# Time mixing: six element-wise passes per chunk moved from VectorE to GpSimd, and the second norm's passes reordered

## The chip, the cores and the metric

The kernel runs on 1 core of a Trainium2 chip. The metric is the device time of one execution in microseconds (us): median of several runs. Engines in the rows: PE is TensorE (matmul), DVE is VectorE, ACT is ScalarE, POOL is GpSimd, SP is SyncE.

## The reference, cut to what matters

The program is a chain of twelve sublayers over an activation of 32 batches, 64 tokens and 256 channels. The change is in the eighth, time mixing (an RWKV attention). It starts with a plain layer norm of the running activation `x`, whose output is `h` in the kernel and `hidden_state` in this cut of the reference:

```python
def _reference_tuple_inner(hidden_state, ln_w, ln_b, Wk, Wv, Wr, Wo, mix_k, mix_v, mix_r, time_decay, current_token_weight):
    residual = hidden_state
    x = _layer_norm(hidden_state, ln_w, ln_b)
    sx = concatenate([zeros, x[:, :-1, :]], axis=1)
    xk, xv, xr = (sx + mix * (x - sx) for mix in (mix_k, mix_v, mix_r))
    r = sigmoid(xr @ Wr.T); k = xk @ Wk.T; v = xv @ Wv.T
    wkv = _wkv(k, v, time_decay, current_token_weight)
    return residual + (r * wkv) @ Wo.T

def step(carry, kv):            # one token of _wkv
    num, den, norm = carry
    kt, vt = kv
    ct = curr_w + kt
    cn = maximum(ct, norm)
    e_prev, e_cur = exp(norm - cn), exp(ct - cn)
    out = (e_prev * num + e_cur * vt) / (e_prev * den + e_cur)
    dpn = decay + norm          # decay = -exp(time_decay)
    new_norm = maximum(dpn, kt)
    e_d, e_k = exp(dpn - new_norm), exp(kt - new_norm)
    return ((e_d * num + e_k * vt, e_d * den + e_k, new_norm), out)
```

The result is added to the running activation `x`, together with `h`.

## The kernel before, in words

Channels lie on the 128 partitions in H2 = 2 halves, the 32 x 64 tokens on the free axis. `time_mixing` (line 1962) works in NCH = 4 chunks of CH = 512 tokens, so that one element-wise pass over a chunk is 128 x 1024. All tensors are f32.

For each chunk c the work is:

- First norm (`ln1`, class `Norm`, line 152), from `k.x` to `k.h`: mean by a matmul (line 171), `centre` on VectorE (line 184, reads PSUM), `squares` on ScalarE (line 197), variance by a matmul (line 179), `inverse` on ScalarE (lines 203 and 205), `scale` on VectorE (line 190). Second norm (`ln2`), the same from `k.h` to `y0`; `affine` on ScalarE (line 2073) writes `yp`.
- `mix` on VectorE: the difference of neighbouring tokens (line 2158, tm_diff), then six instructions (line 2165) that give three mixed inputs, two per projection.
- `project` on TensorE (line 2023): keys, values and gate, each in two halves through one PSUM tile `p_p`; each half waits until ScalarE has copied the same half of the projection before (`keep`, lines 2081, 2085, 2087). The sigmoid of the gate needs two table loads around it (lines 2091 and 2093).
- On VectorE a scan of the maxima (line 2196), four shifts (lines 2201, 2202, 2208, 2209) and the joined maximum (line 2204); on ScalarE an exponential of each shift (lines 2099, 2101). The shifts share one semaphore, which counts four per chunk.
- On VectorE: product 0 of exps and values (line 2214), the scan of the denominator (line 2215), the first norm's scale, the scan of the numerator (line 2220), product 1 (line 2222), two value passes (lines 2225, 2226), `ln_in` (line 2228) and the last sum (line 2230).
- ScalarE takes the logarithm of `ln_in` and its inverse (lines 2138, 2140). VectorE multiplies by the gate (line 2238) and by the inverse into tm_weighted (line 2243).
- `project_out` on TensorE: four records (two matmuls) of the identity by `h` (line 2034), which add the residual, then eight with the output weights (line 2038). VectorE adds the result to `k.x` (line 2171) one chunk later.

A matmul of f32 with 512 columns shows as two records here, so a projection of a chunk (three inputs) is 24 records.

The order of each engine's work is written out by hand in the four blocks of `time_mixing`; instructions of one engine run in that order, and a wait holds back all that stands behind it. Work runs ahead: in the body of chunk c, VectorE mixes chunk c + 1 and runs both norms of chunk c + 2, and TensorE projects chunk c + 1. GpSimd has only three small memsets at the start (lines 2148 to 2150). SyncE loads the weights once. Stage state (tiles `diff`, `yp`, `kp`, `vv`, `rr`, `fo`) has two buffers each.

Of the kernel before, what the change touches and what calls it, by code (L numbers as in the profile page):

```python
# [13 lines left out]
ALU = mybir.AluOpType  # L14
# [6 lines left out]
ts = bass.ts  # L21
# [1940 lines left out]
def time_mixing(k):  # L1962
# [4 lines left out]
    with ExitStack() as ctx:  # L1967
        k.stage += 1
        k.prefix = "tm_"
        sem = semaphores(nc, ctx, k.prefix, "pad affine diff mixed proj kept decay constant joined shifts exps scanned den num "  # L1970
                                            "values weighed ln_in logged inverse fused out added" + Norm.SEMS + Norm.SEMS2)
# [43 lines left out]
        @block.tensor  # L2015
        def _(pe):
            def project(c, n):
                pe.wait_ge(sem["mixed"], 3 * c + n + 1)
                for o in range(H2):
                    if 3 * c + n >= 1:  # L2020
                        pe.wait_ge(sem["kept"], H2 * (3 * c + n - 1) + o + 1)
                    for a in range(H2):
                        mm = pe.matmul(p_p[:, o, :], w[:, n, a, ts(o, P)], mx[:, n, a, :], start=a == 0, stop=a == H2 - 1)
                    mm.then_inc(sem["proj"], 1)

            def mean2(c):
# [24 lines left out]
            for n in range(3):  # L2051
                project(0, n)
            for c in range(NCH):
                if c + 2 < NCH:
                    ln1.var(pe, c + 2)
                if c + 1 < NCH:
                    for n in range(3):
                        project(c + 1, n)
                if c + 3 < NCH:
                    ln1.mean(pe, c + 3)  # L2060
                if c + 2 < NCH:
                    mean2(c + 2)
                    ln2.var(pe, c + 2)
                project_out(c)

        @block.scalar
        def _(act):
# [27 lines left out]
            def exponential(c, n):  # L2095
                act.wait_ge(sem["shifts"], 4 * c + n + 1)
# [22 lines left out]
            for c in range(NCH):  # L2119
                if c + 2 < NCH:  # L2120
                    ln1.squares(act, c + 2)
                if c == 0:
                    act.wait_ge(sem["constant"], 1)
                elif c + 1 < NCH:
                    ln2.inverse(act, c + 1)
                exponential(c, 0)
                if 1 <= c < NCH - 1:
                    affine(c + 1)
# [12 lines left out]
                if c + 2 < NCH:  # L2141
                    ln2.squares(act, c + 2)
# [3 lines left out]
        @block.gpsimd  # L2146
        def _(g):
            g.memset(yp[:, :, :, :, 0:1], 0.0).then_inc(sem["pad"], 1)
            g.memset(kp[:, :, :, :, 0:1], NEG).then_inc(sem["pad"], 1)
            g.memset(run[:, :, 0:1], 0.0).then_inc(sem["pad"], 1)  # L2150

        @block.vector
        def _(v):
            def mix(c):
                v.wait_ge(sem["affine"], c + 1)
                if c >= 2:
                    v.wait_ge(sem["mixed"], 3 * (c - 1))
                v.tensor_tensor(tok(flat(diff[:, c % 2, :, :])), yp[:, c % 2, :, :, 1:S1].rearrange("p o b t -> p (o b) t"),
                                yp[:, c % 2, :, :, 0:S].rearrange("p o b t -> p (o b) t"), ALU.subtract).then_inc(sem["diff"], 1)
# [30 lines left out]
            for c in range(NCH):  # L2190
# [7 lines left out]
                if 1 <= c < NCH - 1:  # L2198
                    ln2.scale(v, c + 1)
# [9 lines left out]
                v.tensor_tensor(tok(expo[3]), keys(c), tok(latest), ALU.subtract).then_inc(sem["shifts"], 1)  # L2209
# [3 lines left out]
                v.wait_ge(sem["kept"], H2 * (3 * c + 2))  # L2213
                v.tensor_tensor(prod[:, 0, :], expo[1], flat(vv[:, c % 2, :, :]), ALU.mult).then_inc(sem["weighed"], 1)
# [12 lines left out]
                v.wait_ge(sem["values"], 4 * c + 2)  # L2227
# [3 lines left out]
                if c + 2 < NCH:  # L2231
                    v.wait_ge(sem["affine"], c + 1)
# [729 lines left out]
```

## Time and profile before

| what | us |
|---|---|
| median of 3 runs | 3419.49 (3416.7 to 3420.05) |
| the profiled execution | 3442.91 |
| its span | 3441.1 |
| PE busy in the span | 2825.3 (82%) |
| DVE busy | 1875.5 (55%) |
| ACT busy | 1394.7 (41%) |
| POOL busy | 921.0 (27%) |

Time mixing takes about 1952 to 2116 us of the span. The shares are means over twelve stages with different limits, so what bounds this one must be read from its own stretch. The chain of work that ended last, as the profile prints it, covers other stages only. The granted clock (PEclk) is TensorE's, as a share of 2.4 GHz.

### The profile page before, as it was taken

The numbers are of one execution on the slowest core, as the hardware profiler recorded it, in microseconds if no ns is written. First come the engines' busy times: TensorE is split into PE (matmuls) and PEld (weight loads), VectorE is DVE, ScalarE is ACT, GpSimd is POOL, SyncE is SP. The second block draws the span as 40 slices with busy tenths as digits, with TensorE's granted clock in tenths as the row PEclk, the third lists the DMA queues.
The fourth block names the chain that finished last, engine by engine and source line by source line (L and its number), as shares of the span: only waits on it lengthen the run. The fifth ranks groups of instructions, "written<-read, shape, count | busy, mean of one in ns | idle before, by whom it ended". The sixth has DMA issues, their size and how long they took to land. (4 is left out here: it accounts for less than half of the span.)

```text
span 3441.1 us, 45938 instructions
## 1 busy us (share of the span) xinstructions
PE 2825.3 (82%) x16624; PEld 1693.8 (49%) x16624; DVE 1875.5 (55%) x2398; ACT 1394.7 (41%) x2464; POOL 921.0 (27%) x733
## 2 busy tenths in 40 slices
PE   7999986899987988789979875587896777785894
PEld 5888864356554647433336432244532333342784
DVE  2333334222258827334479697868755999962341
ACT  3333335121255526222265453465565555530222
POOL 0111100300214512000005300004503999945005
PEclk9999997999998989899989997788998899887997
DMA  6000002311110000200000000000001221222223
GB/s 220 0 0 0 0 7 104 119 43 45 52 40 1 2 20 2 79 1 0 18 1 2 14 0 0 1 19 2 2 25 64 86 85 73 86 74 72 79 83 104
DMA packets 88659, 139.96 MB, mean 41 GB/s; under 512 B 12081, under 2 KB 70449, under 8 KB 83890
## 3 DMA queue, kind: packets, MB, share of 16 engines
q1 hardware_dynamic: 80818, 116.73, 10.0%
q0 software_dynamic: 7680, 20.98, 2.0%
q8 instruction: 114, 1.87, 0.2%
q14 instruction: 47, 0.39, 0.0%
HBM read 105.57 MB, written 32.11 MB: 40 GB/s over the span
## 5 line engine op out<-in xcount | busy, mean ns | idle before, releaser
L2673 PE MATMUL ssm_p_y<-ctxT,ident 128*128 128x512 f32 x512 | 271.3, 685 | 90.0 <-POOL ctxT L2710 82.9
L2719 POOL TENSOR_TENSOR h<-ssm_u,ssp_bc 128x1024 f32<-128x1024 f32 x128 | 297.9, 2361 | 0.0
L2695 ACT ACTIVATE ssm_p_h<-ssp_delta,ss_decay 128x256 f32<-128x256 f32 x512 | 213.7, 463 | 193.7 <-DVE ctxT L2753 165.0
L2673 PEld LDWEIGHTS ssm_p_y<-ctxT,ident 128*128 128x128 f32 x512 | 108.5, 219 | 244.2 <-issue 116.3
L2750 DVE TENSOR_TENSOR_SCAN ssm_p_h<-ssm_p_h,h 128x1024 f32<-128x1024 f32 x88 | 201.2, 2286 | 6.7 <-POOL h L2719 6.4
L559 DVE TENSOR_REDUCE xw_nmax<-xw_p_s 128x8 f32<-128x1024 f32 x32 | 39.2, 1225 | 237.1 <-PE xw_p_s L490 237.1
L580 POOL TENSOR_TENSOR xw_prob<-xw_prob,xw_rsum 128x1024 f32<-128x1024 f32 x32 | 60.7, 1896 | 370.7 <-DVE xw_rsum L566 370.7
L1329 POOL MEMSET ctxT<- 128x512 f32 x3 | 1.6, 526 | 567.2 <-POOLq L61 567.2
L467 PE MATMUL xw_p_q<-h,xw_m_h 128*128 (+1 forms) x1024 | 117.0, 275 | 1.3 <-PEq L61 1.3
L475 PE MATMUL xw_p_q<-xw_u,xw_vo_h 128*128 128x128 f32 x1024 | 117.1, 275 | 0.7 <-ACT xw_u L540 0.7
L475 PEld LDWEIGHTS xw_p_q<-xw_u,xw_vo_h 128*128 128x128 f32 x1024 | 115.6, 192 | 2.2 <-ACT xw_u L540 2.2
L467 PEld LDWEIGHTS xw_p_q<-h,xw_m_h 128*128 128x128 f32 x1024 | 115.6, 192 | 1.7 <-issue 1.7
L2753 DVE TENSOR_TENSOR ctxT<-ssm_p_h,ssp_bc 128x1024 f32<-128x1024 f32 x88 | 107.7, 1224 | 3.0
L1920 ACT ACTIVATE lmm_hidden<-lmm_p_h,vecs 128x512 f32<-128x512 f32 x64 | 43.5, 687 | 153.6 <-PE lmm_p_h L1880 108.1
L1086 POOL DMA_INDIRECT L0f_rows<-L0f_rows_out,L0f_slots x32 | 30.3, 947 | 264.4 <-DMA L0f_rows_out<-L0b_y 250.1
L1086 POOL DMA_INDIRECT L3f_rows<-L3f_rows_out,L3f_slots x48 | 45.4, 947 | 203.2 <-DMA L3f_rows_out<-L3b_y 182.4
L1048 DVE TENSOR_TENSOR L0f_hidden<-L0f_silu,L0b_p_u 128x512 f32<-128x512 f32 x39 | 26.8, 688 | 124.1 <-PE L0b_p_u L992 124.1
L2710 POOL TENSOR_TENSOR ctxT<-ctxT,ssp_bc 128x1024 f32<-128x1024 f32 x40 | 94.1, 2353 | 0.5 <-DVE ctxT L2746 0.4
L2746 DVE TENSOR_TENSOR_SCAN ctxT<-ssm_p_h,h 128x1024 f32<-128x1024 f32 x40 | 91.2, 2281 | 1.4 <-POOL h L2719 1.0
L1949 DVE TENSOR_TENSOR lmm_hidden<-lmm_hidden,lm_weights 128x512 f32<-128x512 f32 x64 | 44.1, 689 | 87.6 <-ACT lmm_hidden L1920 87.6
L1508 POOL TENSOR_TENSOR L1xb_prob<-L1xb_prob,L1xb_rsum 128x896 f32<-128x896 f32 x64 | 65.4, 1042 | 65.5 <-DVE L1xb_rsum L1487 65.5
L1508 POOL TENSOR_TENSOR L3xb_prob<-L3xb_prob,L3xb_rsum 128x896 f32<-128x896 f32 x64 | 65.4, 1042 | 65.2 <-DVE L3xb_rsum L1487 65.2
(650 smaller groups left out, 6771.0 us busy)
## 6 DMA issues: line engine op xcount, KB each, us to landing
ssp_bc<-ss_bc_rows SPq DMA_DIRECT2D x32, 1024.0 KB, 4.7
expert_rows_in<-xw_blank SPq DMA_DIRECT2D x1, 6912.0 KB, 22.0
L3b_x<-expert_rows_in SPq DMA_DIRECT2D x54, 128.0 KB, 2.0
L3f_rows_out<-L3b_y SPq DMA_DIRECT2D x54, 128.0 KB, 1.7
L0b_x<-expert_rows_in SPq DMA_DIRECT2D x39, 128.0 KB, 2.0
L0f_rows_out<-L0b_y SPq DMA_DIRECT2D x39, 128.0 KB, 1.7
L0f_wg<-in_L_ffn_gate SPq DMA_DIRECT2D x9, 512.0 KB, 10.1
L0f_wu<-in_L_ffn_up SPq DMA_DIRECT2D x9, 512.0 KB, 10.0
```

The lines of the kernel that those rows point to most:

```text
L467: mm = pe.matmul(p_q5[:, q % 2, h % 4 // 2, :, h % 2, :], m_h[:, h, a, :], k.h[:, a, ts(i, P)], start=h % 4 == 0 and a == 0, stop=a == H2 ...
L475: mm = pe.matmul(p_q[:, 0, ts(o, P)], vo_h[:, h, ts(o, P)], us[:, h, :], start=h == 0 and o == 0, stop=h == NH - 1, skip_group_check=True)
L580: g.tensor_tensor(prob[:, :, :], prob[:, :, :], bcast(rsum[:, 1, :], 2, S2), ALU.mult).then_inc(sem["normed"], 1)
L1086: g.indirect_dma_start(out=back[:, t % RG, j, :], out_offset=None, in_=rows_out[:, :], in_offset=bass.IndirectOffsetOnAxis(ap=slots[:, j, ...
L1508: scaled = g.tensor_tensor(prob[:, w, :, :, s0:s1], prob[:, w, :, :, s0:s1], bcast(rsum[:, 1, w, m, :, :], 3, s1 - s0), ALU.mult)
L2673: mm = pe.matmul(p_y[:, 2 * half:2 * half + 2, :].rearrange("p e t -> p (e t)"), k.ident[:, :], weighed[s % RING][:, ts(half, CH)], start= ...
L2695: i = act.activation(p_h[:, s % 2, ts(e, CT)], delta[:, e, ts(c, CT)], ACT.Exp, scale=decay[:, 1, E4 * s + e:E4 * s + e + 1])
L2710: g.tensor_tensor(tiles(weighed[s % RING]), tiles(weighed[s % RING]), bcast(bcs[:, s // QUARTER, 1, s % QUARTER, :], 1, E4), ALU.mult).the ...
L2719: g.tensor_tensor(tiles(drive[s % RING]), u[:, c % 2, :, :], bcast(bcs[:, s // QUARTER, 0, s % QUARTER, :], 1, E4), ALU.mult).then_inc(sem ...
L2746: v.tensor_tensor_scan(weighed[s % RING], p_h[:, s % 2, :], drive[s % RING], 0.0, ALU.mult, ALU.add).then_inc(sem["scanned"], 1)
L2750: v.tensor_tensor_scan(p_h[:, s % 2, :], p_h[:, s % 2, :], drive[s % RING], 0.0, ALU.mult, ALU.add).then_inc(sem["scanned"], 1)
L2753: v.tensor_tensor(tiles(weighed[s % RING]), tiles(p_h[:, s % 2, :]), bcast(bcs[:, s // QUARTER, 1, s % QUARTER, :], 1, E4), ALU.mult).then ...
```

## The change: what it does

Six passes run on GpSimd: the difference, the fourth shift (with a semaphore of its own, shift3; the other three keep `shifts`, which now counts three per chunk), both products, a new pass `residual` that adds `h` to `k.x`, and a new pass `gated` that multiplies the gate by the inverse, in place, so that VectorE has one pass (tm_weighted) for the two before. The identity matmuls are gone. The second norm's `centre` moves ahead of the value passes, its `scale` from the next chunk's body to just before tm_weighted; ScalarE's `squares`, `inverse` and `affine` of that norm move around the logarithm and ahead of the gate; TensorE computes the second norm's mean and variance ahead of the first norm's next mean.

```diff
@@ tensor @@
             def project_out(c):
+                pe.wait_ge(sem["fused"], c + 1)
                 if c >= 1:
                     pe.wait_ge(sem["added"], c)
                 for o in range(H2):
-                    pe.matmul(p_y[:, o, :], k.ident[:, :], k.h[:, o, ts(c, CH)], start=True, stop=False, skip_group_check=True)
-                pe.wait_ge(sem["fused"], c + 1)
-                for o in range(H2):
                     for a in range(H2):
...
-                if c + 3 < NCH:
-                    ln1.mean(pe, c + 3)
                 if c + 2 < NCH:
                     mean2(c + 2)
                     ln2.var(pe, c + 2)
+                if c + 3 < NCH:
+                    ln1.mean(pe, c + 3)
                 project_out(c)
@@ scalar @@
                 if c == 0:
                     act.wait_ge(sem["constant"], 1)
-                elif c + 1 < NCH:
-                    ln2.inverse(act, c + 1)
                 exponential(c, 0)
-                if 1 <= c < NCH - 1:
-                    affine(c + 1)
                 exponential(c, 1)
...
                     keep(c + 1, 1)
+                if c + 2 < NCH:
+                    ln2.squares(act, c + 2)
                 act.wait_ge(sem["ln_in"], c + 1)
                 act.activation(expo[2], expo[2], ACT.Ln).then_inc(sem["logged"], 1)
                 act.wait_ge(sem["logged"], c + 1)
                 act.activation(expo[2], expo[2], ACT.Exp, scale=-1.0).then_inc(sem["inverse"], 1)
                 if c + 2 < NCH:
-                    ln2.squares(act, c + 2)
+                    ln2.inverse(act, c + 2)
+                    affine(c + 2)
                 if c + 1 < NCH:
                     gate(c + 1)
@@ gpsimd @@
+            def difference(c):
+                g.wait_ge(sem["affine"], c + 1)
+                if c >= 2:
+                    g.wait_ge(sem["mixed"], 3 * (c - 1))
+                g.tensor_tensor(tok(flat(diff[:, c % 2, :, :])), yp[:, c % 2, :, :, 1:S1].rearrange("p o b t -> p (o b) t"),
+                                yp[:, c % 2, :, :, 0:S].rearrange("p o b t -> p (o b) t"), ALU.subtract).then_inc(sem["diff"], 1)
+
+            def residual(c):
+                g.wait_ge(sem["ln_normed"], c + 1)
+                g.tensor_tensor(k.x[:, :, ts(c, CH)], k.x[:, :, ts(c, CH)], k.h[:, :, ts(c, CH)], ALU.add).then_inc(sem["residual"], 1)
...
+            difference(0)
+            residual(0)
+            residual(1)
+            for c in range(NCH):
+                if c + 1 < NCH:
+                    difference(c + 1)
+                g.wait_ge(sem["joined"], c + 1)
+                g.tensor_tensor(tok(expo[3]), keys(c), tok(latest), ALU.subtract).then_inc(sem["shift3"], 1)
+                g.wait_ge(sem["exps"], 4 * c + 2)
+                g.wait_ge(sem["kept"], H2 * (3 * c + 2))
+                g.tensor_tensor(prod[:, 0, :], expo[1], flat(vv[:, c % 2, :, :]), ALU.mult).then_inc(sem["weighed"], 1)
+                g.wait_ge(sem["exps"], 4 * c + 4)
+                g.tensor_tensor(prod[:, 1, :], expo[3], flat(vv[:, c % 2, :, :]), ALU.mult).then_inc(sem["weighed"], 1)
+                if c + 2 < NCH:
+                    residual(c + 2)
+                g.wait_ge(sem["inverse"], c + 1)
+                g.wait_ge(sem["kept"], H2 * (3 * c + 3))
+                g.tensor_tensor(flat(rr[:, c % 2, :, :]), flat(rr[:, c % 2, :, :]), expo[2], ALU.mult).then_inc(sem["gated"], 1)
@@ vector @@
             def add(c):
                 v.wait_ge(sem["out"], c + 1)
+                v.wait_ge(sem["residual"], c + 1)
...
-                if 1 <= c < NCH - 1:
-                    ln2.scale(v, c + 1)
...
-                v.tensor_tensor(tok(expo[3]), keys(c), tok(latest), ALU.subtract).then_inc(sem["shifts"], 1)
...
-                v.tensor_tensor(prod[:, 0, :], expo[1], flat(vv[:, c % 2, :, :]), ALU.mult).then_inc(sem["weighed"], 1)
...
                 v.tensor_tensor_scan(latest, expo[0], prod[:, 0, :], 0.0, ALU.mult, ALU.add).then_inc(sem["num"], 1)
+                if c + 2 < NCH:
+                    v.wait_ge(sem["affine"], c + 1)
+                    ln2.centre(v, c + 2)
                 v.wait_ge(sem["exps"], 4 * c + 4)
-                v.tensor_tensor(prod[:, 1, :], expo[3], flat(vv[:, c % 2, :, :]), ALU.mult).then_inc(sem["weighed"], 1)
...
-                if c + 2 < NCH:
-                    v.wait_ge(sem["affine"], c + 1)
-                    ln2.centre(v, c + 2)
                 if c >= 1:
                     add(c - 1)
-                v.wait_ge(sem["kept"], H2 * (3 * c + 3))
-                v.wait_ge(sem["values"], 4 * c + 3)
-                v.tensor_tensor(expo[0], expo[0], flat(rr[:, c % 2, :, :]), ALU.mult).then_inc(sem["values"], 1)
-                v.wait_ge(sem["inverse"], c + 1)
-                v.wait_ge(sem["values"], 4 * c + 4)
+                if c + 2 < NCH:
+                    ln2.scale(v, c + 2)
+                v.wait_ge(sem["gated"], c + 1)
+                v.wait_ge(sem["values"], 3 * c + 3)
                 if c >= 2:
                     v.wait_ge(sem["out"], c - 1)
-                v.tensor_tensor(flat(fo[:, c % 2, :, :]), expo[0], expo[2], ALU.mult).then_inc(sem["fused"], 1)
+                v.tensor_tensor(flat(fo[:, c % 2, :, :]), expo[0], flat(rr[:, c % 2, :, :]), ALU.mult).then_inc(sem["fused"], 1)
```

## Rows read from the trace of the kernel before

**Rows 1.** Busy time by stretch: one window per chunk, by the end of its last pass.
```profile
1982.40:2022.20 39.80, 30.28 (x64) 12.85 (x64) 37.16 (x36) 22.14 (x30) 0.00 (x0) 0.91 0.00 0
2022.20:2056.80 34.60, 26.83 (x52) 11.18 (x51) 32.78 (x30) 19.64 (x27) 0.00 (x0) 0.85 0.00 0
2056.80:2086.80 30.00, 19.28 (x39) 7.67 (x38) 29.45 (x28) 15.62 (x21) 0.00 (x0) 0.89 0.00 0
2086.80:2110.00 23.20, 6.09 (x11) 2.61 (x12) 23.01 (x18) 7.91 (x9) 0.00 (x0) 0.65 0.00 0
```

**Rows 2.** Timeline of VectorE: start us, duration us, line, operation, idle before and releaser.
```profile
2000.54 4.07 DVE L2165 SCALAR_TENSOR_TENSOR tm_mixed<-tm_diff,vecs,tm_y 128x512 f32<-128x512 f32 x6
...
2020.93 1.23 DVE L2243 TENSOR_TENSOR tm_weighted<-tm_exps 128x1024 f32<-128x1024 f32 x1
...
2035.20 4.06 DVE L2165 SCALAR_TENSOR_TENSOR tm_mixed<-tm_diff,vecs,tm_y 128x512 f32<-128x512 f32 x6
...
2055.61 1.23 DVE L2243 TENSOR_TENSOR tm_weighted<-tm_exps 128x1024 f32<-128x1024 f32 x1
...
2085.54 1.23 DVE L2243 TENSOR_TENSOR tm_weighted<-tm_exps 128x1024 f32<-128x1024 f32 x1
...
2104.06 1.23 DVE L2228 TENSOR_TENSOR tm_exps<-tm_exps 128x1024 f32<-128x1024 f32 x1
2105.21 1.22 DVE L2230 TENSOR_TENSOR tm_exps<-tm_exps,tm_products 128x1024 f32<-128x1024 f32 x1
...
2108.78 1.23 DVE L2243 TENSOR_TENSOR tm_weighted<-tm_exps 128x1024 f32<-128x1024 f32 x1
```

**Rows 3.** Timeline of TensorE, merged records, same columns as rows 2.
```profile
1985.24 10.54 PE L2023 MATMUL tm_p_p<-tm_mixed,tm_w 128*128 128x512 f32 x24 [2.58 <-DVE tm_mixed L2165]
2000.24 3.78 PE L179 MATMUL tm_ln_p_var<-tm_ln_square,mean_ones 128*128 128x512 f32 x4 [4.46 <-ACT tm_ln_square L197]
2003.82 11.11 PE L2023 MATMUL tm_p_p<-tm_mixed,tm_w 128*128 128x512 f32 x24
...
2036.67 8.80 PE L2023 MATMUL tm_p_p<-tm_mixed,tm_w 128*128 128x512 f32 x13 [5.29 <-DVE tm_mixed L2165]
...
2050.03 1.88 PE L171 MATMUL tm_lm_p_mean<-h,mean_ones 128*128 128x512 f32 x4
...
2107.61 3.62 PE L2034 MATMUL tm_p_y<-h,ident 128*128 128x512 f32 x4 [17.08 <-DVE x L2171]
2111.06 3.60 PE L2038 MATMUL tm_p_y<-tm_weighted,tm_w 128*128 128x512 f32 x8
```

**Rows 4.** Groups of GpSimd by line and shape, whole program.
```profile
L2719 POOL TENSOR_TENSOR h<-ssm_u,ssp_bc 128x1024 f32<-128x1024 f32 x128 | 297.9, 2361 | 0.0
...
L580 POOL TENSOR_TENSOR xw_prob<-xw_prob,xw_rsum 128x1024 f32<-128x1024 f32 x32 | 60.7, 1896 | 370.7 <-DVE xw_rsum L566 370.7
L1508 POOL TENSOR_TENSOR L1xb_prob<-L1xb_prob,L1xb_rsum 128x896 f32<-128x896 f32 x32 | 53.8, 1683 | 65.5 <-DVE L1xb_rsum L1487 65.5
...
L1508 POOL TENSOR_TENSOR L1xb_prob<-L1xb_prob,L1xb_rsum 128x128 f32<-128x128 f32 x32 | 12.9, 402 | 0.0
...
L1493 POOL MEMSET L1xb_vx<- 128x1024 f32 x1 | 1.0, 951 | 65.9 <-POOLq L61 65.9
```

**Rows 5.** State-space stage, timeline of GpSimd, then of VectorE.
```profile
2636.66 2.35 POOL L2701 TENSOR_TENSOR ssm_u<-ssp_delta,ss_xc 128x1024 f32<-128x1024 f32 x1 [61.32 <-POOLq L61]
...
2639.28 9.26 POOL L2719 TENSOR_TENSOR h<-ssm_u,ssp_bc 128x1024 f32<-128x1024 f32 x4
...
2641.73 2.30 DVE L2750 TENSOR_TENSOR_SCAN ssm_p_h<-ssm_p_h,h 128x1024 f32<-128x1024 f32 x1 [5.83 <-POOL h L2719]
...
2645.20 2.28 DVE L2746 TENSOR_TENSOR_SCAN ctxT<-ssm_p_h,h 128x1024 f32<-128x1024 f32 x1
```

**Rows 6.** Timeline of ScalarE: affine of chunk 1, logarithm of chunk 0.
```profile
1997.72 1.52 ACT L2073 ACTIVATE tm_y<-tm_y,vecs 128x512 f32<-128x512 f32 x2
...
2015.94 1.06 ACT L2138 ACTIVATE tm_exps<-tm_exps 128x1024 f32<-128x1024 f32 x1 [3.82 <-DVE tm_exps L2228]
```

More of the change, by code:

```diff
@@ L1969, in time_mixing @@
         k.prefix = "tm_"
-        sem = semaphores(nc, ctx, k.prefix, "pad affine diff mixed proj kept decay constant joined shifts exps scanned den num "
-                                            "values weighed ln_in logged inverse fused out added" + Norm.SEMS + Norm.SEMS2)
+        sem = semaphores(nc, ctx, k.prefix, "pad affine diff mixed proj kept residual decay constant joined shifts shift3 exps scanned den num "
+                                            "values weighed ln_in logged inverse gated fused out added" + Norm.SEMS + Norm.SEMS2)
         s_w = nc.alloc_semaphore("tm_weights_loaded")
@@ L2033, in project_out @@
                 for o in range(H2):
-                    pe.matmul(p_y[:, o, :], k.ident[:, :], k.h[:, o, ts(c, CH)], start=True, stop=False, skip_group_check=True)
-                pe.wait_ge(sem["fused"], c + 1)
-                for o in range(H2):
                     for a in range(H2):
-                        mm = pe.matmul(p_y[:, o, :], w[:, 3, a, ts(o, P)], fo[:, c % 2, a, :], start=False, stop=a == H2 - 1, skip_group_check=True)
+                        mm = pe.matmul(p_y[:, o, :], w[:, 3, a, ts(o, P)], fo[:, c % 2, a, :], start=a == 0, stop=a == H2 - 1)
                 mm.then_inc(sem["out"], 1)
@@ L2095, in exponential @@
             def exponential(c, n):
-                act.wait_ge(sem["shifts"], 4 * c + n + 1)
+                if n < 3:
+                    act.wait_ge(sem["shifts"], 3 * c + n + 1)
+                else:
+                    act.wait_ge(sem["shift3"], c + 1)
                 if n in (0, 3):
@@ L2150, in _ @@
             g.memset(run[:, :, 0:1], 0.0).then_inc(sem["pad"], 1)
+            g.wait_ge(sem["pad"], 1)
+            difference(0)
[16 more added lines that the diff above has]
+                g.tensor_tensor(flat(rr[:, c % 2, :, :]), flat(rr[:, c % 2, :, :]), expo[2], ALU.mult).then_inc(sem["gated"], 1)
         @block.vector
@@ L2154, in mix @@
             def mix(c):
-                v.wait_ge(sem["affine"], c + 1)
[L2156 to L2159, printed above, removed]
                 v.wait_ge(sem["diff"], c + 1)
@@ L2212, in _ @@
                 v.wait_ge(sem["exps"], 4 * c + 2)
-                v.wait_ge(sem["kept"], H2 * (3 * c + 2))
-                v.tensor_tensor(prod[:, 0, :], expo[1], flat(vv[:, c % 2, :, :]), ALU.mult).then_inc(sem["weighed"], 1)
                 v.tensor_tensor_scan(run[:, 1, 1:N + 1], expo[0], expo[1], 0.0, ALU.mult, ALU.add).then_inc(sem["den"], 1)
@@ L2218, in _ @@
                 v.wait_ge(sem["weighed"], 2 * c + 1)
-                v.wait_ge(sem["shifts"], 4 * c + 4)
+                v.wait_ge(sem["shifts"], 3 * c + 3)
                 v.tensor_tensor_scan(latest, expo[0], prod[:, 0, :], 0.0, ALU.mult, ALU.add).then_inc(sem["num"], 1)
+                if c + 2 < NCH:
+                    v.wait_ge(sem["affine"], c + 1)
+                    ln2.centre(v, c + 2)
                 v.wait_ge(sem["exps"], 4 * c + 4)
-                v.tensor_tensor(prod[:, 1, :], expo[3], flat(vv[:, c % 2, :, :]), ALU.mult).then_inc(sem["weighed"], 1)
                 v.wait_ge(sem["den"], c + 1)
@@ L2226, in _ @@
                 v.tensor_tensor(expo[2], expo[2], run[:, 1, 0:N], ALU.mult).then_inc(sem["values"], 1)
-                v.wait_ge(sem["values"], 4 * c + 2)
+                v.wait_ge(sem["values"], 3 * c + 2)
                 v.tensor_tensor(expo[2], expo[2], expo[3], ALU.add).then_inc(sem["ln_in"], 1)
@@ L2230, in _ @@
                 v.tensor_tensor(expo[0], expo[0], prod[:, 1, :], ALU.add).then_inc(sem["values"], 1)
-                if c + 2 < NCH:
-                    v.wait_ge(sem["affine"], c + 1)
-                    ln2.centre(v, c + 2)
                 if c >= 1:
                     add(c - 1)
-                v.wait_ge(sem["kept"], H2 * (3 * c + 3))
-                v.wait_ge(sem["values"], 4 * c + 3)
-                v.tensor_tensor(expo[0], expo[0], flat(rr[:, c % 2, :, :]), ALU.mult).then_inc(sem["values"], 1)
-                v.wait_ge(sem["inverse"], c + 1)
-                v.wait_ge(sem["values"], 4 * c + 4)
+                if c + 2 < NCH:
+                    ln2.scale(v, c + 2)
+                v.wait_ge(sem["gated"], c + 1)
+                v.wait_ge(sem["values"], 3 * c + 3)
                 if c >= 2:
                     v.wait_ge(sem["out"], c - 1)
-                v.tensor_tensor(flat(fo[:, c % 2, :, :]), expo[0], expo[2], ALU.mult).then_inc(sem["fused"], 1)
+                v.tensor_tensor(flat(fo[:, c % 2, :, :]), expo[0], flat(rr[:, c % 2, :, :]), ALU.mult).then_inc(sem["fused"], 1)
             add(NCH - 1)
```

## The prediction

> **What bounds the kernel now.** The change touches one of twelve stages, so I read only that one. The windows come first [rows 1]: from 1982.4 to 2110.0 us VectorE is busy 37.2 of 39.8, 32.8 of 34.6, 29.5 of 30.0 and 23.0 of 23.2 us, one window per chunk; TensorE and ScalarE are far below that, and GpSimd does nothing. VectorE's order of work is the bound of those 128 us. Ahead of them, and in the last 6 us, the stage is a chain of latencies. The timeline of VectorE [rows 2] shows the marks that I count from: the last pass of each chunk (tm_weighted) ends at 2022.2, 2056.8, 2086.8 and 2110.0, so the chunks last 34.7, 29.9 and 23.2 us behind the first. A 1024-wide pass takes 1.22 and the next starts 1.15 behind it; the six mixing passes take 4.0, a scan 2.3 [rows 2, 5]. The timeline of TensorE [rows 3] shows what VectorE's norm passes wait for. The profiled execution took 3442.9 us (span 3441.1) against a median of 3419.5, so it is 0.7% long; differences in us are carried over to the median unchanged, since this stage is 160 us of the span.
>
> **What leaves VectorE.** Five passes per chunk (difference, fourth shift, two products, gate) at 1.14: 5.7 us per chunk, 22.8 in all. That is the most that moving can bring, if each substitute is in time; the idle time left in the four windows [rows 1] is 2.6 + 1.8 + 0.5 + 0.2 = 5.1 more, which is all that the reordering could win. TensorE loses four identity records per chunk (1.9 us); they were hidden, except at the end.
>
> **What comes.** Six GpSimd passes per chunk, 24 in all. A 128x1024 pass with two full inputs takes 2.36 there [rows 4], so 14.2 us per chunk, which fits into 35 us: GpSimd is not the bound by its own time. Its passes are links in chains, though: diff before the mixing passes, product 0 before the numerator scan, product 1 before the last sum, gated before tm_weighted.
>
> **The unknown cost.** Every row in which GpSimd multiplies at length beside a busy VectorE has a VectorE pass with one operand in PSUM: at 2637 us GpSimd alone takes 2.35, and beside the scans its four passes take 9.26 together, the scans 2.30 and 2.28 [rows 5]. So the nearest rows give zero for pass beside pass. But of the 24 VectorE instructions that are left in a full chunk, all but three (two centres and the add) read both operands from SBUF, and no row has such a pair. The other end is that they take turns: the 2.36 in full for every GpSimd pass that meets a dense VectorE. I take the upper end. The rows speak for it in one way: GpSimd's time follows what it reads (0.95 for a memset that reads nothing, 1.90 with one full operand and one value repeated, 2.36 with two [rows 4]), so its reading is what it spends its time on, and a VectorE pass with two SBUF operands needs two streams for all of its 1.22.
>
> The Trainium skill ("SBUF — State Buffer", Who interferes with whom) says that a VectorE instruction with two SBUF inputs contends with a GpSimd instruction that reads SBUF, that the lock is held for the whole instruction, and that a VectorE instruction with at most one SBUF input is free. By that rule the sum is the one for turns below; by the rows alone it would be the one for no cost. The free pairs of [rows 5] agree with the rule, and no row here shows its other half.
>
> **Sum with no cost of pass beside pass.**
>
> Ahead and chunk 0: diff(0) takes 2.36 in place of 1.22, +1.2 on the first projection and on all that ScalarE does behind it, so affine(1), which ended 1999.2 [rows 6], ends 2000.5; diff(1) on GpSimd 2002.9; mixing starts 2003.0 (before 2000.54). TensorE's variance, which waits for ScalarE behind affine(1), ends at 2005.1 in place of 2003.8; then 11.1 for 24 projection records and 1.9 for the second norm's mean [rows 3]: 2018.0. VectorE is there at 2003.0 + 4.0 + 2.2 + 1.1 + 2.2 = 2012.5 and now waits in front of ln2.centre, 5.5 us, with the two value passes queued behind it. Then centre 1.2, two value passes and ln_in 3.4: 2022.6. Behind ln_in the end of the chunk is a chain: Ln and Exp 2.15 [rows 6], gated 2.36, tm_weighted 1.23, handovers 0.3, together 6.1 (ln2.scale fits in). 2028.7 against 2022.2: +6.5.
>
> Chunk 1: centre 1.1, scan 2.3, two shifts 2.3, joined 1.45, shift 1.15: mixing starts 8.35 behind the chunk's start (before 13.1). From mixing's start to the end of the second norm's mean it was 16.7 (2035.20 to 2051.91), of which the first 13 records took 8.8 at a low clock [rows 3]; VectorE has 9.7 us of other work, so it idles 7.0. 8.35 + 16.7 + 1.2 + 3.4 + 6.1 = 35.8 against 34.7: +1.1. At full clock all along, 24 records take 10.3 in place of 13.3, and it is −1.8.
>
> Chunk 2 has no norms. Mixing starts at 7.3, 4.0, 2.2, 2.2 to 15.7, three passes to 19.0, tail 6.1: 25.1 against 29.9: −4.8.
>
> Chunk 3: shifts end 7.3; GpSimd does shift 3 (6.1 to 8.5) and then product 0 to 10.9, which the numerator scan awaits: 13.2, three passes 16.5, tail 6.1: 22.6 against 23.2: −0.6. The tail is where gating on GpSimd hurts: from ln_in's end to tm_weighted's it was 4.7 (2105.3 to 2110.0 [rows 2]).
>
> Output of chunk 3: before, four identity records took 3.62 after a long idle, and the eight behind them 3.60 [rows 3]. With the identity records gone, the eight themselves start cold: 4 at 0.9 and 4 at 0.45, 5.4, against 4.65 from 2110.01 to their end at 2114.66: +0.7.
>
> Sum: 6.5 + 1.1 − 4.8 − 0.6 + 0.7 = +2.9 us.
>
> **Sum with turns.**
>
> Ahead and chunk 0: residual(0) and residual(1) wait for nothing and stand between diff(0) and mixing(0): +4.7, which goes through the projections and ScalarE to affine(1) at 2005.2. diff(1) to 2007.5, shift 3 follows at once to 2009.9 while VectorE stands; product 0 gets in between the first two mixing passes: first mixed tile 2013.7, projections and mean 2026.7, centre, three passes, and a tail of 6.9 (ln2.scale stands until gated is done): 2038.2: +16.0.
>
> Chunk 1: diff(2) ahead of the scan +1.7; shift 3 +2.4, product 0 or 1 +2.4 before the first mixed tile; 16.1 + 13 (between full and low clock) + 1.2 + 3.4 + 6.9 = 40.6: +5.9. The rest, product 1 and residual, falls into the stall for the centre.
>
> Chunk 2: no stall to hide in: 25.1 and four turns (diff, shift 3, both products) 9.4: 34.5: +4.6.
>
> Chunk 3: 22.6, and shift 3 and both products with the den scan between: 28.2: +5.0.
>
> Output +0.7. Sum 32.2 us; that is 29.3 above the first sum, 12.4 of the 24 passes, the others fall into idle time. GpSimd's passes have a fixed part of 0.19 (402 ns for 128 columns, 1683 for 896 [rows 4]) in which nothing is read; over 12 passes −2.2. I take **+30: 3449.5 us**. Its own range is +16 (half of the overlapped time free) to +38 (low clock in both projections, all passes in full): 3436 to 3458.
>
> **Rivals.**
>
> (a) Passes beside each other cost nothing: +2.9, 3422, between 3418 (full clock in chunk 1, −2.9, and in the output, −1.8) and 3425 (a few more handovers). For it: [rows 5]. It is no gain since the second norm's centre now stands in front of the value passes and waits for TensorE, and since gating hangs 2.36 longer behind ScalarE.
>
> (b) Faster: as (a), but TensorE is early enough that the centre waits for nothing, 5.5 + 7.0 us less: 2.9 − 12.5 = −9.6, 3410. It decides at 9.7 us from mixing's start to the mean's end in chunk 1. Against it: it was 16.7, and the fastest projections of [rows 3] took 10.5 for their 24 records, with the mean's 1.9 behind them.
>
> **How the numbers follow.** A measurement of this kernel can tell 0.2%, 6.8 us, from no change. Turns: 0.66, all of it slower. (a): 0.26, all within. (b): 0.08, faster. I give turns two in three because the rows don't exclude them and because no reading of the count brings a real gain: the free case already ends level. The range takes in turns and (a): 3418 to 3458, and leaves out (b) and the few per cent above.
>
> **What would show it.** In the changed kernel's timeline of VectorE: turns, if passes of 1.22 show 2 to 3.5 us or gaps beside tm_exps, tm_products, x and tm_diff of GpSimd, and if GpSimd's own are over 2.4; the centre and the add, with a PSUM operand, should stay at 1.22. An idle time of 5 to 7 us before tm_y<-h,tm_lm_p_mean, released by TensorE, in chunks 0 and 1, shows the stall. tm_weighted released by GpSimd in all chunks shows the tail. VectorE's passes at 1.22 all through with a slower time would make me wrong about the cause; a stage that is 10 us shorter would make me wrong about both.

## The result and the profile after

The changed kernel is slower: 3446.2 us (3443.1 to 3458.9, 4 runs) against 3418.2 (3416.7 to 3420.1, 4 runs), ratio 1.0089 with a 95% interval of 1.0062 to 1.0115, so 28 to 30 us. Timed again beside the experiments, the ratio was 1.0097 (1.0083 to 1.0111). The prediction was +30, 3449.5, in a range of 3418 to 3458.

The profiled execution took 3458.9 us, 16 more than that of before, although the stage alone is 32 longer, so the other stages, which the change does not touch, were 16 shorter in it. The stage itself is what to compare, and it is measured here from a fixed mark, the start of the second norm's centre of chunk 1 (1975.95 before, 1970.09 after), to the end of the last add to `x`: 140.0 us before, 172.1 after, **+32.2**. The page of the changed kernel, busy time per engine in the whole span:

```profile
PE 2828.5 (82%) x16608; PEld 1691.4 (49%) x16608; DVE 1884.5 (55%) x2378; ACT 1395.8 (40%) x2464; POOL 988.1 (29%) x757
```

VectorE executes 20 instructions less than before (2398 then), and yet it is busy 9 us longer. Instructions that leave an engine can't lengthen its busy time, so those that stayed must have grown. How much of the stage that is can be read from two windows over it, from the mark to its end, before and after:

```profile
1975.95:2115.91 139.96, 90.56 (x180) 37.41 (x180) 126.08 (x111) 69.18 (x89) 0.00 (x0) 0.85 0.00 0
1970.09:2142.21 172.12, 92.89 (x164) 37.23 (x164) 134.58 (x91) 69.39 (x89) 66.92 (x24) 0.77 0.00 0
```

(Span, then busy time of PE, PEld, DVE, ACT and POOL with their instructions, then PEclk.) VectorE is busy 126.1 us before and 134.6 after. Twenty passes of 1.14 have left it, which makes 103.3, so the 91 instructions that stayed have grown by 31.3 us. VectorE's idle time grew as well, from 13.9 to 37.5. The +32.2 is therefore −22.8 for the passes that left, +31.3 for growth, and +23.7 for waits. The windows of the changed kernel, one per chunk, with the same columns as [rows 1]:

```profile
1976.50:2033.60 57.10, 34.60 (x65) 13.84 (x64) 42.46 (x31) 23.16 (x32) 23.10 (x9) 0.85 0.00 0
2033.60:2075.10 41.50, 23.95 (x44) 9.60 (x44) 35.49 (x26) 18.79 (x25) 17.22 (x6) 0.79 0.00 1
2075.10:2107.90 32.80, 19.91 (x32) 8.05 (x32) 30.20 (x21) 16.83 (x21) 14.48 (x5) 0.71 0.00 0
2107.90:2135.40 27.50, 5.59 (x8) 2.22 (x8) 22.74 (x14) 6.79 (x8) 12.12 (x4) 0.62 0.00 0
```

VectorE was busy at least 93% of each window before. Now it is 42.5 of 57.1, 35.5 of 41.5, 30.2 of 32.8 and 22.7 of 27.5 us. (The first window starts at diff(0), the three others at the end of tm_weighted.) GpSimd's passes add up to 66.9 us, 2.8 each, though the longest 1024-wide pass of before took 2.41. The timeline of VectorE, columns as in [rows 2]:

```profile
2032.43 1.21 DVE L2262 TENSOR_TENSOR tm_weighted<-tm_exps,tm_gate 128x1024 f32<-128x1024 f32 x1
2033.56 1.21 DVE L184 TENSOR_TENSOR h<-x,tm_ln_p_mean 128x1024 f32<-128x1024 f32 x1
2034.69 3.52 DVE L2222 TENSOR_TENSOR_SCAN tm_maxima<-tm_decay_row,tm_keys 128x1040 f32<-128x1040 f32 x1
...
2041.97 1.23 DVE L2232 TENSOR_TENSOR tm_exps<-tm_maxima,tm_sums 128x1024 f32<-128x1024 f32 x1
...
2043.11 10.15 DVE L2190 SCALAR_TENSOR_TENSOR tm_mixed<-tm_diff,vecs,tm_y 128x512 f32<-128x512 f32 x6
2053.19 2.28 DVE L2236 TENSOR_TENSOR_SCAN tm_sums<-tm_exps 128x1024 f32<-128x1024 f32 x1
...
2056.51 2.28 DVE L2241 TENSOR_TENSOR_SCAN tm_sums<-tm_exps,tm_products 128x1024 f32<-128x1024 f32 x1
2063.51 1.22 DVE L184 TENSOR_TENSOR tm_y<-h,tm_lm_p_mean 128x1024 f32<-128x1024 f32 x1 [4.73 <-PE tm_lm_p_mean L171]
...
2071.71 2.23 DVE L190 TENSOR_TENSOR tm_y<-tm_y,tm_lm_rstd 128x1024 f32<-128x1024 f32 x1 [1.18 <-ACT tm_lm_rstd L205]
2073.86 1.21 DVE L2262 TENSOR_TENSOR tm_weighted<-tm_exps,tm_gate 128x1024 f32<-128x1024 f32 x1
...
2106.64 1.23 DVE L2262 TENSOR_TENSOR tm_weighted<-tm_exps,tm_gate 128x1024 f32<-128x1024 f32 x1 [2.36 <-POOL tm_gate L2180]
...
2134.21 1.23 DVE L2262 TENSOR_TENSOR tm_weighted<-tm_exps,tm_gate 128x1024 f32<-128x1024 f32 x1 [2.36 <-POOL tm_gate L2180]
```

and that of GpSimd:

```profile
1978.44 5.08 POOL L2157 TENSOR_TENSOR x<-x,h 128x1024 f32<-128x1024 f32 x2
...
2029.08 2.35 POOL L2180 TENSOR_TENSOR tm_gate<-tm_gate,tm_exps 128x1024 f32<-128x1024 f32 x1 [8.75 <-ACT tm_exps L2139]
2034.14 1.89 POOL L2152 TENSOR_TENSOR tm_diff<-tm_y 128x1024 f32<-128x1024 f32 x1 [2.71 <-ACT tm_y L2071]
2042.01 3.21 POOL L2170 TENSOR_TENSOR tm_exps<-tm_keys,tm_sums 128x1024 f32<-128x1024 f32 x1 [5.98 <-DVE tm_sums L2228]
...
2045.17 2.81 POOL L2173 TENSOR_TENSOR tm_products<-tm_exps,tm_values 128x1024 f32<-128x1024 f32 x1
2047.94 2.79 POOL L2175 TENSOR_TENSOR tm_products<-tm_exps,tm_values 128x1024 f32<-128x1024 f32 x1
2056.66 4.26 POOL L2157 TENSOR_TENSOR x<-x,h 128x1024 f32<-128x1024 f32 x1 [5.93 <-DVE h L190]
```

Read the two side by side. At 2033.56 VectorE's centre, which has its mean in PSUM, runs beside GpSimd's difference and takes 1.21; the difference takes 1.89. Next is a scan with both operands in SBUF. It starts at 2034.69, GpSimd is done at 2036.03, and the scan's record is 3.52 in place of 2.32: the 1.2 us for which it stood behind GpSimd are counted in it. The six mixing passes, 4.06 before, take 10.15 from 2043.11, while GpSimd goes through the fourth shift and both products, 2.8 to 3.2 each. Three of the six take 2.7 to 2.8 us and the other three 0.74, as before. The residual at 2056.66 takes 4.26: it stands until the numerator scan of 2056.51 is done at 2058.8, then works for 2.1. And where nothing of VectorE's runs (the start of gated at 2029.08) GpSimd takes 2.35; the norm's scale that comes during gated takes 2.23 rather than 1.22 (2071.71), since about 1.1 us of gated were left when it started.

What VectorE waited for between 1976 and 2142 us (line: total us, times, longest):

```profile
DVE tm_y L184 <- PE tm_lm_p_mean L171: 8.6, 2, 4.7
DVE tm_mixed L2190 <- POOL tm_diff L2152: 8.1, 2, 4.4
DVE x L2197 <- PE tm_p_y L2036: 5.6, 1, 5.6
DVE tm_weighted L2262 <- POOL tm_gate L2180: 4.7, 2, 2.4
```

The first line is the wait in front of the second norm's centre, which was 1.7 us in all before. The second and the fourth are links that now pass through GpSimd. The third is the last output projection: TensorE had idled for 22.0 us, and the granted clock was 0.67 from 2135.4 to 2141.0, where it was 0.92 before (2110 to 2116, behind the identity records).

### The profile page after: what moved, and what is told of

Read it like the earlier page. It is cut to its first block and busy times, and to the rows that moved or that the text cites. A ratio compares the mean times of both kernels' runs of the same rounds, so it can differ in the third digit from the quotient of the medians.

```text
span 3457.1 us, 45918 instructions
## 1 busy us (share of the span) xinstructions
PE 2828.5 (82%) x16608; PEld 1691.4 (49%) x16608; DVE 1884.5 (55%) x2378; ACT 1395.8 (40%) x2464; POOL 988.1 (29%) x757
```

## The experiments

"Before beside it" is the kernel before, timed on the same chip beside the experiment. "Stage" is the stage by the mark above, as the difference to before's 140.0.

| kernel | time, median | before beside it | ratio, 95% interval | stage |
|---|---|---|---|---|
| e_after | 3473.0 | 3438.5 | 1.0097, 1.0083 to 1.0111 | +32.3 |
| e_order | 3449.8 | 3438.5 | 1.0032, 1.0020 to 1.0045 | +10.5 |
| e_pool | 3464.2 | 3438.5 | 1.0075, 1.0059 to 1.0091 | +28.0 |
| e_mult | 3469.8 | 3438.5 | 1.0086, 1.0073 to 1.0100 | +30.9 |
| e_memset | 3417.5 | 3418.6 | 0.9998, 0.9988 to 1.0009 | −0.3 |
| e_copy | 3426.4 | 3418.6 | 1.0021, 1.0011 to 1.0030 | +9.9 |
| e_dense | 3433.6 | 3418.6 | 1.0048, 1.0033 to 1.0064 | +21.1 |
| e_gate | 3448.5 | 3418.6 | 1.0090, 1.0074 to 1.0105 | +31.2 |
| e_resid | 3465.2 | 3439.3 | 1.0076, 1.0060 to 1.0092 | +23.7 |
| e_best | 3441.4 | 3439.3 | 1.0008, 0.9997 to 1.0019 | −0.4 |
| e_sub | 3466.5 | 3439.3 | 1.0095, 1.0075 to 1.0115 | +32.9 |

Two theories were set against each other: **turns** (the passes that stayed on VectorE and those of GpSimd run one after the other) and **order** (the new order and the longer links cost the time, and pass beside pass is nearly free).

**e_after**, no edit.

> The changed kernel itself, timed again beside the others. Turns (a VectorE pass with two SBUF operands and a GpSimd pass that reads SBUF run one after the other): 26 to 32 us over the kernel before, as measured. Order (the new waits of the second norm's centre and of the gate are the cause): the same number.

The slowdown is there again, 33 us by the ratio, with the same stage. This run can't tell the two theories apart.

**e_mult.** Nothing of the change is in it: the kernel before, and GpSimd work that nobody waits for.

```diff
@@ gpsimd, behind the memsets (a scratch tile and a semaphore are added, not shown) @@
+            for c in range(NCH):
+                g.wait_ge(sem["joined"], c + 1)
+                for n in range(4):
+                    if 4 * c + n >= 1:
+                        g.wait_ge(sem["idle"], 4 * c + n)
+                    g.tensor_tensor(scr[:, :], k.ctxT[:, 0:1008], k.ctxT[:, N:N + 1008], ALU.mult).then_inc(sem["idle"], 1)
```

> The kernel before, with four multiplications per chunk on GpSimd (two SBUF inputs, 128x1008) that nothing waits for and that start behind the joined maximum, so beside VectorE's mixing passes and scans. Turns: 16 passes of about 2.0, 25 to 35 us over before. Order, or no cost of pass beside pass: within 3 us of before.

Its VectorE and its group of GpSimd instructions:

```profile
1996.32 1.23 DVE L2215 TENSOR_TENSOR tm_exps<-tm_maxima,tm_sums 128x1024 f32<-128x1024 f32 x1
1997.47 3.34 DVE L2216 TENSOR_TENSOR tm_exps<-tm_keys,tm_sums 128x1024 f32<-128x1024 f32 x1
2000.73 3.34 DVE L2165 TENSOR_TENSOR tm_diff<-tm_y 128x1024 f32<-128x1024 f32 x1
2004.10 8.05 DVE L2172 SCALAR_TENSOR_TENSOR tm_mixed<-tm_diff,vecs,tm_y 128x512 f32<-128x512 f32 x6
2012.08 1.21 DVE L2221 TENSOR_TENSOR tm_products<-tm_exps,tm_values 128x1024 f32<-128x1024 f32 x1
```

```profile
L2157 POOL TENSOR_TENSOR tm_scratch<-ctxT 128x1008 f32<-128x1008 f32 x16 | 50.9, 3180 | 123.8 <-DVE tm_sums L2211 122.9
```

Two 1.22 passes take 3.34, the mixing passes 8.05 rather than 4.07, and everything behind them is as before. Each pass of GpSimd makes one VectorE instruction 2.0 to 2.1 longer; GpSimd's own become 3.18 each, as it stands for the next VectorE instruction in between. VectorE's busy time in the stage grows from 126.1 to 159.0 us, 2.06 for each of the sixteen passes. Two of these 32.9 us fall into waits that were there before (11.8 us are left of 13.9), so the stage is 30.9 longer, as turns expected (25 to 35). No link of the kernel passes through these passes, so this is the price of pass beside pass and nothing else. Order has no place for it.

**e_memset, e_copy and e_sub** ask what it is in GpSimd's pass that VectorE waits for. Each is e_mult with the instruction exchanged (e_memset has eight per chunk in place of four, each behind the one before; the signals at the ends of the lines are left out):

```diff
-                    g.tensor_tensor(scr[:, :], k.ctxT[:, 0:1008], k.ctxT[:, N:N + 1008], ALU.mult)
+                    g.memset(scr[:, :], 1.0)                                    # e_memset, eight per chunk
+                    g.tensor_copy(scr[:, :], k.ctxT[:, 0:1008])                 # e_copy
+                    g.tensor_tensor(scr[:, :], k.ctxT[:, 0:1008], k.ctxT[:, N:N + 1008], ALU.subtract)  # e_sub
```

> As e_mult, with eight memsets of 128x1008 per chunk in place of the multiplications: GpSimd writes as long, and reads nothing. Turns on the reads: within 3 us of before. Turns of whole instructions whatever they read: 32 passes of 0.9, about 28 us over before.

> As e_mult, with four copies of 128x1008 per chunk (one SBUF input). Turns per instruction: the cost is the copies' own duration, some 1 us each, 12 to 20 us over before. If it takes a second read on GpSimd's side as well: within 3 us of before.

> As e_mult with subtractions in place of the multiplications. The difference pass of the changed kernel took 1.89 us alone and the gated product 2.34. If VectorE waits for as long as GpSimd's instruction works: 16 times about 1.5, 20 to 28 us over before, less than with multiplications. If the wait is by the operands alone: the same as with multiplications, about 31.

e_memset, the two passes behind the joined maximum, and GpSimd's seven memsets in that window:

```profile
2014.87 1.22 DVE L2217 TENSOR_TENSOR tm_exps<-tm_keys,tm_sums 128x1024 f32<-128x1024 f32 x1
2016.00 1.22 DVE L2166 TENSOR_TENSOR tm_diff<-tm_y 128x1024 f32<-128x1024 f32 x1
...
2013.75 6.91 POOL L2158 MEMSET tm_scratch<- 128x1008 f32 x7 [27.61 <-DVE tm_sums L2212]
```

e_copy, the same shift, the mixing passes, and GpSimd's four copies:

```profile
1980.49 2.04 DVE L2216 TENSOR_TENSOR tm_exps<-tm_keys,tm_sums 128x1024 f32<-128x1024 f32 x1
...
1984.53 5.47 DVE L2172 SCALAR_TENSOR_TENSOR tm_mixed<-tm_diff,vecs,tm_y 128x512 f32<-128x512 f32 x6
...
1979.38 7.43 POOL L2157 COPY tm_scratch<-ctxT 128x1008 f32<-128x1008 f32 x4 [44.44 <-DVE tm_sums L2211]
```

e_sub, the same two passes as above in e_mult:

```profile
1989.50 3.34 DVE L2216 TENSOR_TENSOR tm_exps<-tm_keys,tm_sums 128x1024 f32<-128x1024 f32 x1
1992.76 3.34 DVE L2165 TENSOR_TENSOR tm_diff<-tm_y 128x1024 f32<-128x1024 f32 x1
```

Thirty-two memsets cost nothing: VectorE's passes stay at 1.22, and the memsets take 0.94 on average, where one of 128x1024 in another stage took 0.95 [rows 4]. A copy makes a VectorE pass 0.82 longer (2.04 rather than 1.22), a two-input pass 2.12. So VectorE waits for GpSimd's reading: nothing for none, 0.8 for one stream, 2.1 for two. The copies cost 9.9 us in the stage, below the 12 that was expected at the least, and so in neither of the two ranges. VectorE's busy time grows by 12.1 us (126.1 to 138.2), 0.76 for each copy, and the other 2.3 us is wait that was there before: in chunk 0, where VectorE had waited 0.9 us for `affine` and 1.4 in front of the centre, the end comes only 0.5 later, and in the other three 2.9 to 3.2. The subtraction costs what the multiplication does, as expected of a wait that goes by the operands; that it would be cheaper, the other expectation, read off the short difference pass, did not come.

**e_order and e_pool** split the change in two.

```diff
@@ e_order, to the kernel before: tensor, scalar, vector @@
-                if c + 3 < NCH:
-                    ln1.mean(pe, c + 3)
                 if c + 2 < NCH:
                     mean2(c + 2)
                     ln2.var(pe, c + 2)
+                if c + 3 < NCH:
+                    ln1.mean(pe, c + 3)
...
-                    ln2.inverse(act, c + 1)
...
-                    affine(c + 1)
...
+                    ln2.squares(act, c + 2)
...
-                    ln2.squares(act, c + 2)
+                    ln2.inverse(act, c + 2)
+                    affine(c + 2)
...
-                    ln2.scale(v, c + 1)
...
+                    v.wait_ge(sem["affine"], c + 1)
+                    ln2.centre(v, c + 2)
...
-                    v.wait_ge(sem["affine"], c + 1)
-                    ln2.centre(v, c + 2)
...
+                    ln2.scale(v, c + 2)
@@ e_pool, to the changed kernel: the same lines the other way @@
...
```

> The reordering of the second norm's passes alone, all element-wise passes on VectorE. Turns: only the wait in front of the centre is left, about 5 us in chunks 0 and 1, some of it won back by the earlier scale: 5 to 12 us over before, with VectorE's mixing passes at 0.75 each. Order: most of the slowdown, 20 us or more over before.

> The six passes on GpSimd alone, with the norms where they were before. Turns: VectorE loses five passes of 1.14 per chunk and gains six waits of about 2.1: 20 to 30 us over before, and nothing that hides them. Order: without the new waits the passes that left VectorE show as a gain, 5 us or more under before.

e_order, what VectorE waited for, from 1970 to 2120 us:

```profile
DVE tm_y L184 <- PE tm_lm_p_mean L171: 13.8, 3, 5.5
DVE tm_y L190 <- ACT tm_lm_rstd L205: 5.9, 3, 2.4
```

The centre waits three times, 5.5 us at the longest (one of them is in the start-up), and the scale 5.9 in all. The order costs 10.5 us of stage by itself, +0.32% in time (5 to 12 were expected with turns); the passes by themselves 28.0 (20 to 30 expected). Together they would make 38.5, and the change makes 32.2. The 6 us between them lie in chunks 0 and 1 for the most part (3.7 and 1.7), where the order opened waits; that turns fall into these is read from this sum and not shown by a run of its own.

Turns fit both, and order fits neither. e_order lacks most of the slowdown. e_pool has no new wait of the norm but keeps the longer links, and these are not free: VectorE waits in its stage for 34.2 us (13.9 before), among them these:

```profile
DVE tm_mixed L2191 <- POOL tm_diff L2153: 11.7, 4, 4.4
DVE tm_weighted L2263 <- POOL tm_gate L2181: 8.3, 4, 2.4
```

The new waits, 20.3 us, are less than the 22.8 us of passes that left VectorE, so by these windows waits of this length alone would have left it 2.5 us under before (an estimate, since without turns the waits would not be the same). What makes it +28.0 is that VectorE's other instructions grow by 30.4 us (busy 133.7 of 167.9, with 20 instructions fewer).

**e_dense, e_gate and e_resid** undo one group of passes each.

```diff
@@ e_dense: the fourth shift and both products in VectorE's order of before (additions not shown) @@
...
-                g.tensor_tensor(tok(expo[3]), keys(c), tok(latest), ALU.subtract).then_inc(sem["shift3"], 1)
...
-                g.tensor_tensor(prod[:, 0, :], expo[1], flat(vv[:, c % 2, :, :]), ALU.mult).then_inc(sem["weighed"], 1)
...
-                g.tensor_tensor(prod[:, 1, :], expo[3], flat(vv[:, c % 2, :, :]), ALU.mult).then_inc(sem["weighed"], 1)
@@ e_gate: two multiplications on VectorE, as before (additions not shown) @@
...
-                g.tensor_tensor(flat(rr[:, c % 2, :, :]), flat(rr[:, c % 2, :, :]), expo[2], ALU.mult).then_inc(sem["gated"], 1)
@@ e_resid: identity matmuls, as before (additions not shown) @@
-            residual(0)
-            residual(1)
...
-                    residual(c + 2)
```

> The changed kernel with the fourth shift and both products back on VectorE; difference, residual and gated stay on GpSimd. Turns: 12 passes of 1.14 for 12 waits of about 2.1, so 9 to 15 us under the changed kernel. Without turns: VectorE has 13.7 us more to do, of which the wait in front of the centre hides a part, so 0 to 8 us over the changed kernel.

> The changed kernel with the gate multiplied on VectorE again. Turns and the chain at a chunk's end: the second norm's scale isn't held up (1 us in chunks 0 and 1) and the last pass starts 1.3 us earlier in chunks 2 and 3: 3 to 7 us under the changed kernel. If gated costs nothing where it stands: within 2 us of it.

> The changed kernel with the residual added by TensorE's identity matmuls again, and no residual pass on GpSimd. Turns: the two passes that stood ahead of the first mixing passes are gone, 4 to 5 us less in front of chunk 0; those of chunks 0 and 1 fell into the wait for the centre and save nothing; the output of chunk 3 about 1 us less. In all 4 to 7 us under the changed kernel. Without turns: within 2 us of it.

e_dense is 11.1 us of stage under the changed kernel, and 1.0048 against 1.0097 in time (17 us, with intervals of 5 us on each side): 12 passes fewer on GpSimd, and the kernel is faster with 13.7 us more work on VectorE. Turns had expected 9 to 15 us less, and no turns 0 to 8 us more. The shorter links are not the reason: VectorE's idle time in the stage goes only from 37.5 to 35.6 us, while its busy time falls from 134.6 to 125.5, in spite of the work that came back. e_resid is 8.5 us of stage under the changed kernel (expected 4 to 7), 7 us by the two ratios, which is hardly more than their intervals of 5 us each. Of these, 6.4 are gained up to the end of chunk 0, 0.4 in chunk 1 and 1.8 at the output. The mixing passes of chunk 0 in e_resid:

```profile
1983.98 4.07 DVE L2188 SCALAR_TENSOR_TENSOR tm_mixed<-tm_diff,vecs,tm_y 128x512 f32<-128x512 f32 x6 [3.71 <-POOL tm_diff L2154]
```

4.07, against 8.13 in the changed kernel, where the two residual passes of 1978.44 (5.08 us for both) ran beside them. e_gate is a miss: only 1.0 of stage, where turns had expected 3 to 7 less, and nothing that the timing can tell. It lies in the other range, within 2 us of the changed kernel. Its end of chunk 0:

```profile
2019.71 1.22 DVE L190 TENSOR_TENSOR tm_y<-tm_y,tm_lm_rstd 128x1024 f32<-128x1024 f32 x1 [2.31 <-ACT tm_lm_rstd L205]
2020.86 1.22 DVE L2257 TENSOR_TENSOR tm_exps<-tm_exps,tm_gate 128x1024 f32<-128x1024 f32 x1
2022.18 1.23 DVE L2262 TENSOR_TENSOR tm_weighted<-tm_exps 128x1024 f32<-128x1024 f32 x1
```

The last pass starts 1.0 and 1.1 us earlier in chunks 2 and 3, as expected. But in chunk 0 it starts 0.9 later, since the norm's scale still waits for ScalarE until 2019.7, and then two passes are queued behind it rather than one; the output took 0.8 longer. So gated costs something where it stands, and the two gains are nearly lost again elsewhere.

**e_best** is the kernel before with two of the moves, on the idea that they fill the small gaps.

```diff
@@ to the kernel before: tensor as in e_order, and vector @@
-                if 1 <= c < NCH - 1:
-                    ln2.scale(v, c + 1)
                 v.wait_ge(sem["scanned"], c + 1)
                 v.tensor_tensor(tok(expo[0]), prev, now, ALU.subtract).then_inc(sem["shifts"], 1)
+                if 1 <= c < NCH - 1:
+                    ln2.scale(v, c + 1)
```

> The kernel before with two moves and nothing on GpSimd: TensorE takes the second norm's mean ahead of the first norm's next mean, and VectorE scales the second norm behind the first shift. Both theories: the idle 1.4, 1.3 and 0.4 us of VectorE in chunks 0 to 2 shrink, 1 to 3 us under before, which is below what the timing can tell.

It gains 0.4 us of stage, less than the 1 to 3 that were expected, and nothing in time. Its list of waits has a line that was not there before:

```profile
DVE h L184 <- PE tm_ln_p_mean L171: 2.4, 1, 2.4
```

The first norm's centre of chunk 3 now waits 2.4 us, as its mean stands behind the second norm's variance on TensorE. The gap moved. No kernel here beats the one before.

## Why the prediction was right, point by point

The forecast, turns, was what happened: +30 was put down, and the two timings gave 28 to 30 and 33. The sum for the stage before the 2.2 for GpSimd's fixed part was taken off, 32.2, is also what the profile shows. That they agree to the tenth is luck, since errors of both signs cancel:

| stretch | sum with turns | measured |
|---|---|---|
| ahead and chunk 0 | +16.0 | +17.3 |
| chunk 1 | +5.9 | +6.7 |
| chunk 2 | +4.6 | +2.9 |
| chunk 3 | +5.0 | +4.3 |
| output | +0.7 | +0.9 |

(Measured between the ends of tm_weighted: 41.4, 32.8 and 27.6 us for chunks 1 to 3, against 34.7, 29.9 and 23.2 [rows 2].)

- **The price of a turn** was put at 2.36 in the sum and is 2.0 to 2.1 in the records. The 0.19 that the prediction took off for the fixed part, over 12 passes, is most of the difference. In chunk 2, where nothing hides the turns, the price accounts for it: the records grow by 1.5 for diff and 6.1 for the other three, 7.6 rather than 9.4, and the chunk is 1.7 us shorter than worked out.
- **Where the turns fall.** The prediction let one product in between the first mixing passes and, in chunk 1, had the other fall into the stall for the centre. In chunks 0 and 1 both products and most of the shift fell beside the six mixing passes, which took 10.1. The first mixed tile was not late for that: TensorE's projections start 37.9 us behind the mark in chunk 0 (37.8 worked out) and 14.9 into chunk 1 (16.1 worked out). That residual(0) and residual(1) double the first mixing passes was right (8.13 for 4.07).
- **The projections** were mis-sized, and that is most of why chunks 0 and 1 are longer than the sum. With the second norm's mean they were put at 13.0 us and took 14.0 and 14.8:

```profile
2007.98 12.26 PE L2023 MATMUL tm_p_p<-tm_mixed,tm_w 128*128 128x512 f32 x24 [2.67 <-DVE tm_mixed L2190]
2020.08 1.88 PE L171 MATMUL tm_lm_p_mean<-h,mean_ones 128*128 128x512 f32 x4
...
2048.58 13.11 PE L2023 MATMUL tm_p_p<-tm_mixed,tm_w 128*128 128x512 f32 x24 [7.72 <-DVE tm_mixed L2190]
2061.53 1.88 PE L171 MATMUL tm_lm_p_mean<-h,mean_ones 128*128 128x512 f32 x4
```

TensorE had idled 2.7 and 7.7 us for the first mixed tile, and the granted clock was 0.67 and 0.50 in the first 4 us behind it. Before, chunk 0's projections followed on the variance without a pause (0.87 in their first 5.2 us). In chunk 1 the 1.8 us lost here outweigh the 1.2 by which the tile was early.
- **The wait in front of the centre** came out at 3.9 and 4.7 us. The 5.5 and 7.0 were worked out without turns; e_order, which has none, shows 5.5 and 4.8, with product 0 (1.1) back in front of both and the difference on VectorE. The first agrees by the same working; of the second a good 1 us was too much. That the residual would fall into this wait was right: its 4.26 us held up nothing, and e_resid gained 0.4 in chunk 1.
- **The tail.** tm_weighted waits for gated 2.36 us in chunks 2 and 3, and the norm's scale stands behind gated in 0 and 1 (2.23), as worked out. By e_gate this tail costs 1 us in each of the last two chunks and 1 over all, where its expectation had 3 to 7.
- **The output** projection in a cold start: eight records in 5.46 us against 5.4 expected.
- **The two ends.** The free end, +2.9, had the order cost nearly nothing over all, because VectorE's 22.8 us of removed work paid for it. e_order shows +10.5 for the order with that work still there. The free end itself was not tried. An estimate from the two windows over the stage: without the 31.3 us of growth the changed kernel would stand 0.9 over before if its waits stayed as they are, and some more if waits took up part of that, so +2.9 is not contradicted. Rival (b), a centre that waits for nothing, did not happen: it waited 3.9 and 4.7 us.

The sentence that decided was that the nearest rows were of another kind: there VectorE had an operand in PSUM. Taken at their face, [rows 5] would have given +2.9. The Trainium skill's rule ("SBUF — State Buffer", Who interferes with whom) is borne out in all three parts that runs here touch: two SBUF inputs against a reading GpSimd pass wait (1.22 to 3.34), a pass with one SBUF input doesn't (the centre at 2033.56, over the 0.6 us that it shares with GpSimd's difference, and the scans of [rows 5]), and a GpSimd pass that only writes doesn't matter (e_memset).

## What to carry to other kernels

Before moving an element-wise pass from VectorE to GpSimd, count the SBUF operands of the VectorE instructions that will run beside it. Where they have two, the pass has not left the queue: here it cost up to 2.1 us of VectorE's time in place of 1.14 (31.3 us over the stage for 22.8 saved), and the longer links cost waits on top. Work on GpSimd that is free beside PSUM-reading passes says nothing of the same work beside SBUF-reading ones. A busy time that rises while the instruction count falls is the sign to look for.

## What the runs showed of the hardware

- Turns are by whole instructions, from both sides. With both engines dense, GpSimd takes one pass for each VectorE instruction, so a 0.74 us mixing pass (2.8 when it has to stand) is as good a target as a 2.3 us scan (4.3), and GpSimd's records swell to 2.8 for short VectorE instructions and to 4.3 for scans.
- The price depends on the streams that GpSimd reads (128x1008, for one VectorE pass of 1.22 us with two SBUF inputs): none 0.00, one 0.82, two 2.12 us, and the operation makes no difference (multiplication and subtraction both 3.34 for a 1.22 pass).
- The difference pass took 1.89 us alone where other two-input passes take 2.35. Its two operands are the same tile shifted by one token; that this is the reason was not tried, and the operation is not it (e_sub).
